# Moving the low parts of a split-precision matmul 64 bytes aside in on-chip memory

## The chip, the core and the metric

The kernel runs on one core of one Trainium2 chip. The metric is the time of one execution on the device, in microseconds (us); less is better. Float32 products are made on TensorE out of three cheaper passes each, so that TensorE is used far more than the arithmetic alone would ask.

## The reference

A "macaron" block on x of 4096 tokens by 256 channels: half of a feed-forward part, a retention part with 8 heads, and the same feed-forward part again, each behind a layer norm and added to its input.

```python
def ffn(x):                       # x: layer-normed, 4096 x 256
    x_prev = shift_by_one_token(x)
    xr = mu_r * x + (1 - mu_r) * x_prev
    xk = mu_k * x + (1 - mu_k) * x_prev
    r = sigmoid(xr @ W_r.T)
    k = relu(xk @ W_k.T) ** 2
    return r * (k @ W_v.T)

x = x + 0.5 * ffn(layernorm(x))
x = x + retention(layernorm(x) @ Wq, ... @ Wk, ... @ Wv) @ Wo   # causal, decay per head
x = x + 0.5 * ffn(layernorm(x))
```

## The kernel before

**Blocks and stages.** The tokens are cut into 16 blocks of 256 (two tiles of 128). Each block goes through the stages FFN1, RET and FFN2. The stages of different blocks run at the same time: in the loop `for i in range(6, 16)` TensorE works on FFN1 of blocks i-2 and i-1, on RET of i-4 and i-3 and on FFN2 of i-6 and i-5. The order of the work on every engine is written out by hand; one pass of that loop is called an iteration here.

**Splitting.** A float32 operand `a` is stored as `a_hi` (rounded to float32r, the format of the three passes) and `a_lo = a - a_hi`. ScalarE (ACT) writes the high parts, VectorE (DVE) and GpSimd (POOL) the low parts. One product is the sum of three passes: high by high, low of one by high of the other, high by low. The weights are split once, at the start.

**The two forms of a product.** Every matmul has an operand that is loaded into the array first (the stationary one, a LDWEIGHTS of 128 columns, engine PEld in the profile) and one that is streamed through it (256 columns). Both are float32 in memory, so a load reads 512 bytes of each partition and a stream 1024.
- `half_T` (line 1097) loads the weight `w` and streams the operand `x`. It makes `hidden`, `query` and `key`.
- `half_rows` (line 1105) loads `x` and streams `w`. It makes `gate`, `ffn_out`, `value` and `retention_out`.

Each call of either is a run of six matmuls: two halves `g` of the contraction, three passes each. Calls of one form often follow each other, so that the trace shows runs of 6 or 12.
Behind "psum<-" the profile prints the streamed operand first and the loaded one second: `psum<-xa_hi,w_hi` streams `xa_hi` through `w_hi`.

**The first and the last block.** Block 0 of FFN1 and block 15 of FFN2 (and its output projection of retention) use plain float32 matmuls on `w_f32`, `xkT`, `xrT`, `sqT` and `o_last` (lines 1268 to 1315). Line 1330 is a warm-up on a tensor of zeros, which it loads and streams; line 1334 is a run of ten matmuls that load and stream `w_hi` and keep the clock up near the end.

**Where the tensors lie.** `sb` allocates them one behind another in a partition's memory, in the order of the declarations, each at the next multiple of 32 bytes. The sizes are multiples of 128 bytes for all large tensors but `xnT` (2056 bytes); small ones between them move what follows. Added up from the declarations, the start addresses are, modulo 128 bytes:

| tensors | before | after the change |
|---|---|---|
| `w_f32`, `w_hi` | 0 | 0 |
| `w_lo` | 0 | 64 |
| `ident`, `zeros`, `decay`, `decq`, `deck` | 32 | 96 |
| `x0`, `x1`, `x2`, `y` | 0 | 64 |
| `xn`, `dT`, `xkT`, `xrT`, `sqT`, `qT`, `kT`, `vrow`, `krow`, `attn`, `o_last` | 64 | 0 |
| `xk_hi`, `xr_hi`, `ka_hi`, `xa_hi`, `o_hi` | 64 | 64 |
| `xk_lo`, `xr_lo`, `ka_lo`, `xa_lo`, `o_lo` | 64 | 0 |

Of the kernel before, what the change touches and what calls it, by code (L numbers as in the profile page):

```python
# [8 lines left out]
F32R = mybir.dt.float32r  # L9
# [5 lines left out]
G = D // P  # L15
TILES = 2
BT = TILES * P
# [7 lines left out]
def build(nc, x_in, weights, mu_in, ident_in, decay_in, decq_in, deck_in, gstate_in, x_out):  # L25
# [5 lines left out]
    with ExitStack() as ctx:  # L31
        def sb(name, shape, dt=F32):
            return ctx.enter_context(nc.sbuf_tensor(name, [P] + shape, dt))

        def ring(name, count, shape, dt=F32):

            return [sb(f"{name}_{k}", shape, dt) for k in range(count)]
# [11 lines left out]
        W_R, W_K, W_V, W_Q, W_KEY, W_VAL, W_O = range(7)  # L49
        w_f32 = [sb(f"w_f32_{w}", [G, D]) for w in range(7)]  # L50
        w_hi = [sb(f"w_hi_{w}", [G, D], F32R) for w in range(7)]
        w_lo = [sb(f"w_lo_{w}", [G, D], F32R) for w in range(7)]
        mu = sb("mu", [2, G])
        ident = sb("ident", [P])
# [25 lines left out]
        def ffn(name, count, shape, dt=F32):  # L80
            return {f: ring(f"{name}_{f}", count, shape, dt) for f in (FFN1, FFN2)}
# [1 line left out]
        xnT = ffn("xnT", 2, [G, BT + 1])  # L83
        dT = ffn("dT", 2, [G, BT])
        xkT, xrT = ffn("xkT", 2, [G, BT]), ffn("xrT", 2, [G, BT])
        xk_hi, xk_lo = ffn("xk_hi", 2, [G, BT], F32R), ffn("xk_lo", 2, [G, BT], F32R)
        xr_hi, xr_lo = ffn("xr_hi", 2, [G, BT], F32R), ffn("xr_lo", 2, [G, BT], F32R)
        reluT, sqT = ffn("reluT", 1, [G, BT]), ffn("sqT", 1, [G, BT])
        ka_hi, ka_lo = ffn("ka_hi", 1, [G, BT], F32R), ffn("ka_lo", 1, [G, BT], F32R)
        rgate, gatedx = ffn("rgate", 1, [TILES, D]), ffn("gatedx", 1, [TILES, D])  # L90


        xa_hi, xa_lo = sb("xa_hi", [G, BT], F32R), sb("xa_lo", [G, BT], F32R)
        qT, kT = sb("qT", [G, BT]), sb("kT", [G, BT])
        vrow, krow = sb("vrow", [TILES, D]), sb("krow", [TILES, D])
        attn = [sb(f"attn_{r}", [G, TILES, P]) for r in range(HG)]
        state = [sb(f"state_{c}", [G, HD]) for c in range(TILES)]
        state_dec = [sb(f"state_dec_{c}", [G, HD]) for c in range(TILES)]
        o_hi, o_lo = sb("o_hi", [G, BT], F32R), sb("o_lo", [G, BT], F32R)

        o_last = sb("o_last", [G, BT])

        psum = ctx.enter_context(nc.psum_tensor("psum", [P, 8, 512], F32))
        bank = [psum[:, b, :] for b in range(8)]

        def halves(b):
            return bank[b].rearrange("p (g t) -> p g t", g=2)
# [73 lines left out]
        def signal(whole, name, f, part):  # L181
            return half_done[name] if part == 0 else whole[f]
# [37 lines left out]
        def splits(f, n):  # L220

            return max(n - 1, 0) if f == FFN1 else n
# [859 lines left out]
        def _(pe):  # L1082
# [9 lines left out]
            def half_T(b, w, hi, lo, m):  # L1092

                cols = slice(m * P, (m + 1) * P)
                passes = [(w_hi[w], hi), (w_lo[w], hi), (w_hi[w], lo)]
                for j, (g, (wt, xt)) in enumerate([(g, p) for g in range(G) for p in passes]):
                    mm = pe.matmul(halves(b)[:, m, :], wt[:, g, cols], xt[:, g, :], start=(j == 0), stop=(j == 5))  # L1097
                return mm
# [9 lines left out]
            def weight_split(n, w):  # L1108

                if n == 0 or (n == 1 and w in (W_R, W_K, W_V)):  # L1110
                    pe.wait_ge(w_hi_ready[w], 1)
                    pe.wait_ge(w_lo_ready[w], 1)

            def hidden(f, n, half):
                if half == 0:
                    pe.wait_ge(xk_lo_ready[f], splits(f, n + 1))
                    weight_split(n, W_K)
                mm = half_T(B_HID[f], W_K, xk_hi[f][n % 2], xk_lo[f][n % 2], half)
                if half == 1:
                    mm.then_inc(hid_psum[f], 1)  # L1120
# [17 lines left out]
            def query(n, half):  # L1138
                if half == 0:
                    pe.wait_ge(xa_lo_ready, n + 1)  # L1140
                    weight_split(n, W_Q)
                mm = half_T(B_Q, W_Q, xa_hi, xa_lo, half)
                if half == 1:
                    mm.then_inc(q_psum, 1)

            def key(n, half):
                if half == 0:
                    pe.wait_ge(xa_lo_ready, n + 1)
                    weight_split(n, W_KEY)
                mm = half_T(B_KEY, W_KEY, xa_hi, xa_lo, half)  # L1150
                if half == 1:
                    mm.then_inc(key_psum, 1)
# [79 lines left out]
            def hidden_in_parts(f, n, step):  # L1232

                g = min(step, 1)
                pe.wait_ge(signal(xk_lo_ready, "xk_lo", f, g), splits(f, n + 1) if g != 0 else 1)
                if step == 0:
                    weight_split(n, W_K)
                hi, lo = xk_hi[f][n % 2], xk_lo[f][n % 2]
                for m in range(2) if step == 0 else [step - 1]:
                    b, cols = (B_HID_1[f] if m else B_HID[f]), slice(m * P, (m + 1) * P)  # L1240
                    for j, (wt, xt) in enumerate(((w_hi[W_K], hi), (w_lo[W_K], hi), (w_hi[W_K], lo))):
                        mm = pe.matmul(halves(b)[:, m, :], wt[:, g, cols], xt[:, g, :], start=(g == 0 and j == 0), stop=(g == 1 and j == 2))
                if step > 0:
                    mm.then_inc(signal(hid_psum, "hid", f, step - 1), 1)
# [504 lines left out]
```

## Time and profile before

| | |
|---|---|
| median of 3 runs | 336.15 us (335.98 to 336.43) |
| the profiled execution's own time | 336.06 us |
| its span, from the first to the last instruction | 334.3 us |
| TensorE (PE) busy | 323.9 us (97%) |
| weight loads (PEld) busy | 303.2 us (91%) |
| VectorE (DVE) busy | 298.0 us (89%) |
| ScalarE (ACT) busy | 206.4 us (62%) |
| GpSimd (POOL) busy | 136.5 us (41%) |

The span is what the engines' records cover; the execution's own time holds some 1.8 us more around it. A matmul's record starts when its streaming starts and ends after its results have passed the array, so records of consecutive matmuls overlap, and PE is "busy" whenever one of them is in flight. What one matmul costs is therefore the distance from its start to the next one's, not its duration. The granted clock of TensorE was 1.000 over the span.

### The profile page before, as it was taken

Reading aid. Unit: us, or ns where it says so; the run is one execution under the profiler, and the core shown is the slowest. Engines: PE = TensorE matmul, PEld = TensorE weight load, DVE = VectorE, ACT = ScalarE, POOL = GpSimd, SP = SyncE. Lnnn points to the kernel's source line nnn. Section 1 sums busy time; section 2 is a strip of 40 time slices with the busy share of each in tenths; the row PEclk is TensorE's granted clock in tenths of the full one; section 3 lists DMA queues with packets and bytes.
Section 4 is the critical chain, followed back from the end, with each engine's and each line's share of the span. In section 5 each row is a group of like instructions: output and inputs, shape, how many; then the busy total and the mean of one; then the engine's idle time right before and its main releaser. Section 6 shows DMA issues by size and latency. Waiting matters only on the chain.

```text
span 334.3 us, 11273 instructions
## 1 busy us (share of the span) xinstructions
PE 323.9 (97%) x4252; PEld 303.2 (91%) x4252; DVE 298.0 (89%) x699; ACT 206.4 (62%) x414; POOL 136.5 (41%) x242
## 2 busy tenths in 40 slices
PE   7889999999999999999999999999999999999995
PEld 7679989999899999999999999989999999999893
DVE  4998899999998999899999989999997989888883
ACT  3685665774757586575758657575866738164542
POOL 3476563708153350716345070634516114333320
PEclk9999999999999999999999999999999999999999
DMA  7611010102002010200202020011001000000001
GB/s 243 240 35 33 3 31 3 35 2 64 4 1 65 2 65 4 63 4 3 64 2 64 4 64 2 10 58 34 2 2 34 2 33 4 31 2 33 5 31 63
DMA packets 11556, 12.08 MB, mean 36 GB/s; under 512 B 1008, under 2 KB 11120, under 8 KB 11504
## 3 DMA queue, kind: packets, MB, share of 16 engines
q1 hardware_dynamic: 11072, 11.18, 10.7%
q8 instruction: 34, 0.56, 0.7%
q10 hardware_dynamic: 432, 0.20, 0.2%
q14 instruction: 18, 0.15, 0.1%
HBM read 7.18 MB, written 4.19 MB: 34 GB/s over the span
## 4 chain that ended last, share of the span: by engine, by line
PE 90%; DVE 5%; issue 2%; ACT 0%; POOL 0%; DVEq 0%; ACTq 0%; POOLq 0%
PE psum L1105 39%; PE psum L1097 26%; PE psum L1089 6%; PE psum L1176 5%; PE psum L1208 5%; PE psum L1195 3%; PE psum L1166 2%; PE psum L1221 2%; PE psum L1298 2%; DVE xrT L800 1%; DVE w_lo L175 1%; PE psum L1315 1%; PE psum L1279 1%; DVE dT L780 0%; DVE state_dec L845 0%
## 5 line engine op out<-in xcount | busy, mean ns | idle before, releaser
L234 POOL TENSOR_TENSOR xr_lo<-xrT,xr_hi 128x512 fp32r<-128x512 f32 x27 | 45.4, 1695 | 118.9 <-ACT xr_hi L427 118.9
L396 ACT ACTIVATE xn<-x,shift,rstd 128x256 f32<-128x256 f32 x92 | 49.7, 590 | 2.7 <-POOL shift L323 2.6
L836 DVE TENSOR_TENSOR attn<-psum,decay 128x512 f32<-128x512 f32 x64 | 42.2, 683 | 6.6 <-PE psum L1176 5.9
L466 ACT ACTIVATE kT<-psum 128x512 f32<-128x512 f32 x16 | 9.6, 598 | 51.9 <-PE psum L1097 51.9
L1105 PE MATMUL psum<-w_hi,xr_hi 128*128 128x256 f32 x120 | 37.6, 314 | 0.5 <-issue 0.5
L700 DVE BATCH_NORM_STATS2 stats<-x 128x6 f32<-128x256 f32 x94 | 34.9, 413 | 3.5 <-DMA x<-in_x 3.4
L1097 PE MATMUL psum<-xa_hi,w_hi 128*128 128x256 f32 x128 | 36.4, 284 | 0.4 <-DVE xa_lo L814 0.3
L1097 PE MATMUL psum<-xa_lo,w_hi 128*128 128x256 f32 x128 | 35.6, 278 | 0.0
L1097 PE MATMUL psum<-xa_hi,w_lo 128*128 128x256 f32 x128 | 35.6, 278 | 0.0
L1105 PE MATMUL psum<-w_hi,ka_hi 128*128 128x256 f32 x120 | 35.4, 295 | 0.1
L319 POOL TENSOR_TENSOR rstd<-var_eps,exponent 128x2 f32<-128x2 f32 x47 | 33.4, 710 | 3.7 <-DVE var_eps L711 3.7
L1097 PE MATMUL psum<-xk_hi,w_hi 128*128 128x256 f32 x120 | 34.7, 289 | 0.2 <-issue 0.2
L1105 PE MATMUL psum<-w_hi,ka_lo 128*128 128x256 f32 x120 | 33.6, 280 | 0.0
L1105 PE MATMUL psum<-w_hi,xr_lo 128*128 128x256 f32 x120 | 33.6, 280 | 0.0
L1105 PE MATMUL psum<-w_lo,ka_hi 128*128 128x256 f32 x120 | 33.6, 280 | 0.0
L1105 PE MATMUL psum<-w_lo,xr_hi 128*128 128x256 f32 x120 | 33.5, 279 | 0.0
L1097 PE MATMUL psum<-xk_lo,w_hi 128*128 128x256 f32 x120 | 33.3, 278 | 0.0
L1097 PE MATMUL psum<-xk_hi,w_lo 128*128 128x256 f32 x120 | 33.2, 277 | 0.0
L1089 PE MATMUL psum<-ident,xn 128*128 128x128 f32 x188 | 28.2, 273 | 2.0 <-DVE xn L717 1.0
L435 ACT ACTIVATE reluT<-psum 128x512 f32<-128x512 f32 (+1 forms) x32 | 18.7, 584 | 17.5 <-PE psum L1097 16.1
L800 DVE SCALAR_TENSOR_TENSOR xrT<-dT,mu,xnT 128x256 f32<-128x256 f32 x62 | 29.0, 508 | 0.0
L315 POOL TENSOR_TENSOR var_eps<-moments,eps 128x2 f32<-128x2 f32 x46 | 16.7, 363 | 25.0 <-DVE moments L706 24.3
(122 smaller groups left out, 1040.7 us busy)
## 6 DMA issues: line engine op xcount, KB each, us to landing
x<-in_x SPq DMA_DIRECT2D x15, 256.0 KB, 2.9
x_out<-y SPq DMA_DIRECT2D x15, 256.0 KB, 3.0
w_f<-in_w SPq DMA_DIRECT2D x7, 256.0 KB, 6.1
decay<-in_decay SPq DMA_DIRECT2D x1, 512.0 KB, 6.8
decq<-in_decq SPq DMA_DIRECT2D x1, 256.0 KB, 6.5
deck<-in_deck SPq DMA_DIRECT2D x1, 256.0 KB, 6.5
x_out<-y SPq DMA_DIRECT2D x2, 128.0 KB, 1.7
x<-in_x ACTq DMA_DIRECT2D x1, 128.0 KB, 2.8
```

Source lines behind the costliest of these rows:

```text
L234: engine.tensor_tensor(xr_lo[f][n % 2][:], xrT[f][n % 2][:], xr_hi[f][n % 2][:].bitcast(F32), ALU.subtract).then_inc(xr_lo_ready[f], 1)
L319: pool.tensor_tensor(rstd[s][n % 2][:], var_eps[s][n % 2][:], exponent[:], ALU.pow).then_inc(rstd_ready[s], 1)
L396: act.activation(xn[s][n % 2][:, t, :], x[n % len(x)][:, t, :], ACT.Identity, bias=shift[s][n % 2][:, t:t + 1], scale=rstd[s][n % 2][:, t: ...
L435: act.activation(reluT[f][0][:, s, :], halves(b)[:, s, :], ACT.Relu).then_inc(signal(relu_ready, "relu", f, part), 1)
L700: dve.bn_stats(stats[s][n % 2][:, t, :], x[n % len(x)][:, t, :]).then_inc(stats_ready[s], 1)
L800: dve.scalar_tensor_tensor(out=xrT[f][n % 2][:, g, :], in0=dT[f][n % 2][:, g, :], scalar=mu[:, 0, g:g + 1], in1=xnT[f][n % 2][:, g, 0:BT], ...
L836: dve.tensor_tensor(attn[r][:], bank[B_SCORES[r]].rearrange("p (g c i) -> p g c i", g=G, c=TILES), decay[:, r, :, :].unsqueeze(2).broadcas ...
L1089: mm = pe.transpose(halves(B_T[s])[:, g, t * P:(t + 1) * P], xn[s][n % 2][:, t, g * P:(g + 1) * P], ident[:])
L1097: mm = pe.matmul(halves(b)[:, m, :], wt[:, g, cols], xt[:, g, :], start=(j == 0), stop=(j == 5))
L1105: mm = pe.matmul(halves(b)[:, t, :], xt[:, g, cols], wt[:, g, :], start=(j == 0), stop=(j == 5))
L1176: mm = pe.matmul(bank[B_SCORES[r]][:, group * P:(group + 1) * P], kT[rows, g, c * P:(c + 1) * P], qT[rows, g, c * P:(c + 1) * P], start=Tr ...
L1208: mm = pe.matmul(bank[B_OT + g][quadrant(g, r), c * P:(c + 1) * P], vrow[:, c, cols], attn[r][:, g, c, :], start=(first and c == 0), stop= ...
```

## The change

Three pads of 64 bytes (`gap_lo`, `gap_hi`, `gap_split`) are put between declarations, and the high and low parts of the operands are declared together, behind everything else. All `w_lo` then start 64 bytes off `w_hi`, and all operands' low parts 64 bytes off their high parts. In `half_T` and in `hidden_in_parts` the pass with `w_lo` comes first. The number of instructions and their sizes stay as they are.

```diff
         w_hi = [sb(f"w_hi_{w}", [G, D], F32R) for w in range(7)]
+
+        gap_lo = sb("gap_lo", [16])
         w_lo = [sb(f"w_lo_{w}", [G, D], F32R) for w in range(7)]
...
-        xk_hi, xk_lo = ffn("xk_hi", 2, [G, BT], F32R), ffn("xk_lo", 2, [G, BT], F32R)
-        xr_hi, xr_lo = ffn("xr_hi", 2, [G, BT], F32R), ffn("xr_lo", 2, [G, BT], F32R)
         reluT, sqT = ffn("reluT", 1, [G, BT]), ffn("sqT", 1, [G, BT])
-        ka_hi, ka_lo = ffn("ka_hi", 1, [G, BT], F32R), ffn("ka_lo", 1, [G, BT], F32R)
...
-        xa_hi, xa_lo = sb("xa_hi", [G, BT], F32R), sb("xa_lo", [G, BT], F32R)
...
-        o_hi, o_lo = sb("o_hi", [G, BT], F32R), sb("o_lo", [G, BT], F32R)
 
         o_last = sb("o_last", [G, BT])
+
+
+        gap_hi = sb("gap_hi", [16])
+        xk_hi, xr_hi, ka_hi = ffn("xk_hi", 2, [G, BT], F32R), ffn("xr_hi", 2, [G, BT], F32R), ffn("ka_hi", 1, [G, BT], F32R)
+        xa_hi, o_hi = sb("xa_hi", [G, BT], F32R), sb("o_hi", [G, BT], F32R)
+        gap_split = sb("gap_split", [16])
+        xk_lo, xr_lo, ka_lo = ffn("xk_lo", 2, [G, BT], F32R), ffn("xr_lo", 2, [G, BT], F32R), ffn("ka_lo", 1, [G, BT], F32R)
+        xa_lo, o_lo = sb("xa_lo", [G, BT], F32R), sb("o_lo", [G, BT], F32R)
...
             def half_T(b, w, hi, lo, m):
 
                 cols = slice(m * P, (m + 1) * P)
-                passes = [(w_hi[w], hi), (w_lo[w], hi), (w_hi[w], lo)]
+                passes = [(w_lo[w], hi), (w_hi[w], hi), (w_hi[w], lo)]
...
-                    for j, (wt, xt) in enumerate(((w_hi[W_K], hi), (w_lo[W_K], hi), (w_hi[W_K], lo))):
+                    for j, (wt, xt) in enumerate(((w_lo[W_K], hi), (w_hi[W_K], hi), (w_hi[W_K], lo))):
```

## Rows read from the trace of the kernel before

**Rows 1.** The page, part 1: busy time of each engine, its share and instructions.

```profile
PE 323.9 (97%) x4252; PEld 303.2 (91%) x4252; DVE 298.0 (89%) x699; ACT 206.4 (62%) x414; POOL 136.5 (41%) x242
```

**Rows 2.** The page, part 4: the chain that ended last, by engine.

```profile
PE 90%; DVE 5%; issue 2%; ACT 0%; POOL 0%; DVEq 0%; ACTq 0%; POOLq 0%
```

**Rows 3.** Busy time in three windows: stretch, its length, engine busy (instructions).

```profile
0.00:64.40 64.40, 58.54 (x666) 53.52 (x666) 54.86 (x137) 39.25 (x78) 34.57 (x69) 1.00 0.26 81
64.40:278.70 214.30, 214.30 (x2910) 202.97 (x2906) 199.60 (x468) 141.67 (x285) 85.81 (x151) 1.00 0.09 26
278.70:334.30 55.60, 51.03 (x681) 46.68 (x680) 43.53 (x97) 25.50 (x53) 16.11 (x24) 1.00 0.07 25
```

**Rows 4.** The chain in time order, one iteration: start us, us, engine, line, count.

```profile
142.49 0.91 PE psum L1105 x6
...
143.84 1.38 PE psum L1105 x12
...
146.25 0.90 PE psum L1105 x6
...
148.16 0.88 PE psum L1105 x6
149.05 1.36 PE psum L1097 x12
150.41 1.42 PE psum L1105 x12
151.82 0.71 PE psum L1097 x6
152.53 0.69 PE psum L1105 x6
153.23 0.68 PE psum L1097 x6
153.91 1.42 PE psum L1105 x12
155.32 1.42 PE psum L1097 x12
156.74 0.44 PE psum L1089 x4
157.18 0.71 PE psum L1105 x6
157.89 0.68 PE psum L1097 x6
...
159.01 0.69 PE psum L1097 x6
159.69 0.71 PE psum L1105 x6
```

**Rows 5.** The same view near the end: the run of line 1334.

```profile
320.95 1.20 PE psum L1334 x10
```

**Rows 6.** Whole span, line 1105 alone, then line 1097: stretch, PE, PEld.

```profile
0.00:334.30 334.30, 156.00 (x1092) 136.23 (x1092) 1.00 0.12 36
...
0.00:334.30 334.30, 101.27 (x744) 91.98 (x744) 1.00 0.12 36
```

**Rows 7.** Waits of DVE within the iteration: us in total, times, longest.

```profile
DVE krow L829 <- PE psum L1166: 0.3, 1, 0.3
DVE attn L836 <- PE psum L1176: 0.2, 1, 0.2
```

**Rows 8.** Timeline: start us, us, engine; a matmul and the load beside it.

```profile
150.72 0.28 PE L1105 MATMUL psum<-w_lo,ka_hi 128*128 128x256 f32 x1
150.72 0.19 PEld L1105 LDWEIGHTS psum<-w_hi,ka_lo 128*128 128x128 f32 x1
```

**Rows 9.** Timeline near the start: the warm-up of line 1330.

```profile
7.00 1.73 PE L1330 MATMUL psum<-zeros 128*128 128x128 f32 x14
```

## The prediction

> **What bounds the kernel now.** I read the page first. PE is busy for 323.9 of 334.3 us [rows 1], and the chain that ended last is PE for 90% [rows 2]. Busy PE is no proof of PE at its peak, so I cut the span into a beginning, a middle and an end: in the middle, 64.4 to 278.7 us, PE is in flight for every one of the 214.30 us, while before and after it has gaps, 58.54 of 64.40 and 51.03 of 55.60 us [rows 3]. The middle repeats: the same piece of the chain comes back each 19.40 us, 214.30 / 19.40 = 11.05 iterations. So the time of the middle is the number of matmuls times the distance between their starts, and nothing that another engine does counts until PE has to wait for it.
>
> What a matmul costs is then the thing to read, and the chain in time order gives it for each run: its pieces go from one matmul's end to the next one's [rows 4]. The reader is to see that there are two paces for the very same shapes. The run of 12 at 149.05 takes 1.36 us, 0.1133 each; the run of 12 at 150.41 takes 1.42 us, 0.1183 each. I call them the short and the long pace. Neither belongs to one form: line 1097 (w loaded) has the short one at 149.05, 153.23 and 157.89 and the long one at 151.82 and 155.32; line 1105 (w streamed) the short one at 152.53 and the long one at 153.91. A pace lasts over a boundary from 1105 to 1097: 148.16 to 149.05 short, 150.41 to 151.82 long, 152.53 to 153.23 short, 153.91 to 155.32 long; 157.18 to 157.89 is the exception. At every boundary from 1097 straight to 1105 it turns over: 149.05 to 150.41 short to long, 151.82 to 152.53 long to short, 153.23 to 153.91 and 159.01 to 159.69 short to long [rows 4].
>
> Now the addresses. While matmul k streams, the load for k+1 reads; both start together, as at 150.72 [rows 8]. Before the change all w parts start at 0 modulo 128 and all x parts at 64. Inside a run one of them is streamed and the other loaded, so the two start in different halves of 128 bytes. Only at a boundary between the forms do both start in the same half: (64, 64) from 1097 to 1105, (0, 0) from 1105 to 1097. The pace turns over just where the pair is (64, 64). And the one run in which streamed and loaded operand are the same bytes throughout, line 1334, goes at 1.20 / 10 = 0.120 us each, the longest of all for this shape [rows 5]. That is the evidence that the half matters. It is no proof: at (0, 0) boundaries the pace mostly stays.
>
> **What the change does to this.** With the new addresses and pass order the pairs (streamed, next loaded) are, for 1097, (hi 64, w_hi 0), (hi 64, w_hi 0), (lo 0, w_lo 64), and for 1105 (w_hi 0, hi 64), (w_lo 64, lo 0), (w_hi 0, hi 64). At the boundaries 1097 ends with lo at 0 and 1105 begins with hi at 64; 1105 ends with w_hi at 0 and 1097 begins with w_lo at 64. So the start halves differ in every pair, at the boundaries too. Inside runs they differed before, so nothing is won there directly. What I expect to go is the turn-over at boundaries.
>
> The price, per iteration, against 0.68 per six [rows 4]: 150.41 gives back 0.06, 151.82 0.03, 152.53 0.01, 153.91 0.06, 155.32 0.06, 159.69 0.03, together 0.25 us. All six lie behind a turn-over; without it they inherit the short pace that 148.16 and 159.01 have. The long starts behind other kinds of matmul have no such cause and I leave them as they are: 142.49 and 146.25 (0.91 and 0.90 against 0.88 at 148.16, so 0.03 and 0.02), 143.84 (0.02), 157.18 (0.03), together 0.10 us. The rows are rounded to 0.01, so either sum may be 0.03 off.
>
> Times how many iterations: lines 1105 and 1097 have 1092 + 744 = 1836 such matmuls [rows 6], at 120 in an iteration 15.3 iterations' worth. 11.05 of them are in the middle, where PE never waits and every saved nanosecond counts. The other 4.25 lie at the ends, where PE is in flight for 91% of the time and part of a saving goes into waits; between a half and 0.91 I take 0.7, which is 3.0. That makes 14.0 iterations, and 0.25 x 14.0 = 3.5 us.
>
> The rest I cost at nothing, with these bounds. **The cover:** a faster PE brings nearer what DVE owes it. In the iteration DVE waits for PE for 0.3 + 0.2 = 0.5 us [rows 7]; that is how far an iteration can shrink before DVE's order sets it, and 0.25 is half of it. If PE gained more, the next thing late would be DVE's scores and key rows, and PE would begin to wait for attn and xa_lo. **The plain float32 matmuls** of the first and last blocks (64 instructions) now stream and load from one half, where they had two. At worst each loses what line 1334 loses against the short pace, 0.120 - 0.1133 = 0.007, in all 0.4 us; but the warm-up, which loads and streams the same zeros, goes at about (1.73 - 0.28) / 13 = 0.112 us [rows 9], for 128 columns of plain float32, no more than 256 columns of a pass take here, so I see no price for a same-half pair there. I take 0. **Pairs among the other tensors** (transposes, scores, retention) move by 64 bytes together and keep their relative places: 0. **The pass order** only swaps two loads, and both weight parts are waited for before the run in any case: 0. **Vector, scalar and DMA work** sees starts that are moved by 64 bytes; DVE's 0.5 us and the loads issued blocks ahead cover it: 0.
>
> Sum: the profiled execution would take 336.06 - 3.5 = 332.6 us; it lies 0.09 us under the median of the runs, so the median would be 336.15 - 3.5 = 332.6 us.
>
> **Rules that speak against it.** PE is slowed by something between its two readers, as the two paces for one shape show [rows 4]. The Trainium skill says otherwise: "TensorE: Matmul & The Clock Gate", section "Step-by-step: what each phase is for", gives TensorE two independent read ports, one for the streamed operand and one for the loads, and "SBUF — State Buffer", section "SBUF: two separate sides", has contention only on the port pair that VectorE and GpSimd share. By that rule a move of 64 bytes changes nothing and the time stays 336.15 us; it leaves the two paces unexplained, so I give it little.
>
> **The rivals.**
> - *Every run gets the short pace*, those behind other kinds of matmul too (0.35 per iteration). For it: those starts may depend on the same halves. Against it: their first pairs are as before. 0.35 x 14.0 = 4.9 us, 331.3 us. Chance 0.10.
> - *A pace under 0.1133.* Transposes go at 0.44 / 4 = 0.110 [rows 4]. If 0.1133 still holds a conflict, 120 x 0.0033 = 0.4 us more per iteration would come free, 0.75 in all, above DVE's 0.5 us, which caps it: 0.5 x 14.0 = 7 us, 329.1 us. Against it: the halves inside runs differ already. Chance 0.06.
> - *The alternation costs something.* Now the half of the streamed operand changes inside runs. 152.53, right behind a change, has 0.01 over 153.23; at 0.01 for each six, 20 times an iteration, 0.2 of the 0.25 is eaten: 0.05 x 14.0 = 0.7 us, 335.5 us. Chance 0.10.
> - *Nothing changes*: the pace is set by the relative timing in which a run starts, and addresses 64 bytes apart are no matter. For it: the exception at 157.18 and the (0, 0) boundaries. 336.15 us. Chance 0.09.
> - *Slower.* What turns the pace over is not the equal halves but the move of the streamed operand from one half to the other; at 1097 to 1105 it goes from 64 to 0. Then the change puts such a move into every group of three passes, and the long pace prevails. Of the 120 matmuls of an iteration 66 are at the long pace now; it decides against the change from more than 66 on. With all of them there, the other 54 lose 0.005 each, 0.27 us, times 14.0: 3.8 us, 339.9 us; at line 1334's pace 120 x 0.0067 - 0.35 = 0.45 us, 342.5 us. Against it: from 0 to 64, at 1105 to 1097, the pace stays. Chance 0.21, a third of it under 338.
>
> **How the numbers follow.** My own case (turn-overs gone, 332.6 us) has the remaining 0.44. A run of this kernel can be told from no change above some 0.2%, 0.7 us. Faster by more: 0.44 + 0.10 + 0.06 + half of the eaten gain, 0.05, makes 0.65. Within 0.2%: 0.05 + 0.09 = 0.14. Slower: 0.21. The range goes from 331.0 us, just under the case of all runs short with the rounding of its sum, to 338.0 us; outside are the lower pace (0.06) and two thirds of the slower case (0.14). My own case alone spans 331.9 to 333.3 us: the rounding of its sum, 0.03 x 14, and the share taken at the ends, 0.5 to 0.91.
>
> **What the profile after would show.** The chain in time order again: if I am right, the runs that answer to those at 150.41, 151.82, 153.91, 155.32 and 159.69 take 0.68 per six and not 0.71, those at 142.49, 146.25 and 157.18 stay, and an iteration takes 19.15 us and not 19.40, with PE still without waits. DVE's waits for PE shrink by some 0.25 us. If all runs show 0.71 or more, the slower case holds; if the long ones are as many but elsewhere, the pace is a matter of timing. If a pace under 0.68 appears, look for PE's waits on DVE. I would be wrong above all if the state at which a run starts is set by something that the new addresses move as well, since one short or long start is then inherited by nine runs behind it.

## The result and the profile after

The changed kernel takes 339.25 us (median of 4 runs, 338.92 to 339.37) against 336.29 us for the kernel before beside it: a ratio of 1.0083, 95% interval 1.0070 to 1.0096. It is slower by 0.8%. The forecast was 332.6 us, with a range up to 338.0; the time lies above it. Ratios compare undisturbed executions: one of the 11 of the run `pads_256` below took 453.43 us at a granted clock of 0.657 and has no part in its ratio.

The profiled execution took 339.33 us, its span is 337.5 us, 3.2 more than before. In the windows of the three parts and of one iteration (stretch, length, busy time of PE, PEld, DVE, ACT and POOL), the middle has grown most, and PE is still in flight for all of it, as in [rows 3]. An iteration takes 19.63 us and not 19.40:

```profile
0.00:65.00 65.00, 59.83 (x694) 54.74 (x698) 55.30 (x137) 39.56 (x79) 34.85 (x69) 1.00 0.25 80
65.00:281.50 216.50, 216.50 (x2902) 205.22 (x2888) 199.50 (x467) 141.47 (x284) 85.54 (x151) 1.00 0.09 25
281.50:337.50 56.00, 51.53 (x681) 47.13 (x680) 43.50 (x97) 25.48 (x53) 16.23 (x24) 0.99 0.07 25
143.26:162.89 19.63, 19.63 (x268) 18.64 (x264) 18.24 (x43) 12.95 (x28) 8.00 (x15) 1.00 0.10 28
```

The chain in time order of that iteration answers, run by run, to [rows 4] (line 1110 is 1105 of before, 1102 is 1097, 1094 is 1089):

```profile
143.72 0.92 PE psum L1110 x6
...
145.08 1.41 PE psum L1110 x12
...
147.53 0.91 PE psum L1110 x6
...
149.44 0.92 PE psum L1110 x6
150.36 1.42 PE psum L1102 x12
151.78 1.41 PE psum L1110 x12
153.19 0.71 PE psum L1102 x6
153.90 0.70 PE psum L1110 x6
154.61 0.71 PE psum L1102 x6
155.32 1.41 PE psum L1110 x12
156.73 1.42 PE psum L1102 x12
...
158.59 0.71 PE psum L1110 x6
159.29 0.71 PE psum L1102 x6
...
160.44 0.72 PE psum L1102 x6
161.16 0.70 PE psum L1110 x6
```

There is no run of 0.68 left. The reader can add up where the time went, after minus before: 143.72 +0.01, 145.08 +0.03, 147.53 +0.01, 149.44 +0.04, 150.36 +0.06, 151.78 -0.01, 153.90 +0.01, 154.61 +0.03, 155.32 -0.01, 159.29 +0.03, 160.44 +0.03, 161.16 -0.01, the others 0. That is 0.22 us of the 0.23 by which the iteration grew. Ten iterations in a row take 19.627 us each, 0.227 more than 19.40, and 0.227 times the 14.0 iterations of the prediction is 3.2 us, all of the span's growth. What ran at the long pace still does; everything that ran at the short one has lost it.

### The profile page after: what moved, and what is told of

It reads as the page before. It is cut to its first block, busy times and chain, and to the rows that moved or that the text cites. A ratio compares the mean times of both kernels' runs of the same rounds, so it can differ in the third digit from the quotient of the medians.

```text
span 337.5 us, 11273 instructions
## 1 busy us (share of the span) xinstructions
PE 327.9 (97%) x4252; PEld 307.1 (91%) x4252; DVE 298.3 (88%) x699; ACT 206.5 (61%) x414; POOL 136.6 (40%) x242
## 4 chain that ended last, share of the span: by engine, by line
PE 91%; DVE 5%; issue 2%; ACT 0%; POOL 0%; DVEq 0%; POOLq 0%; ACTq 0%
PE psum L1110 39%; PE psum L1102 26%; PE psum L1094 6%; PE psum L1181 5%; PE psum L1213 4%; PE psum L1200 3%; PE psum L1171 2%; PE psum L1226 2%; PE psum L1303 2%; DVE w_lo L180 1%; PE psum L1320 1%; PE psum L1284 1%; DVE xrT L805 1%; DVE stats L705 0%; DVE state_dec L850 0%
## 5 line engine op out<-in xcount | busy, mean ns | idle before, releaser
L1102 PE MATMUL psum<-xa_hi,w_lo 128*128 128x256 f32 x128 | 36.7, 287 | 0.4 <-DVE xa_lo L819 0.4
L1102 PE MATMUL psum<-xk_hi,w_lo 128*128 128x256 f32 x120 | 35.2, 293 | 0.2 <-issue 0.2
L1102 PE MATMUL psum<-xk_hi,w_hi 128*128 128x256 f32 x120 | 33.7, 281 | 0.0
```

## The experiments

**Theories.** A, that of the prediction: a matmul is held up when streamed and next loaded operand start in one half of 128 bytes. B: it is held up when the streamed operand moves from one half to the other between matmuls. C: the pace is set by timing, by waits and the other engines. D, which came up after experiment 5: the short pace needs an operand pair that keeps its places, modulo 256 bytes, from matmul to matmul.

**1. The parts of the change.** The pads and declarations of the change with the old pass order, and the new pass order on the old layout:

```diff
 # pads_only: the changed kernel, but
-                passes = [(w_lo[w], hi), (w_hi[w], hi), (w_hi[w], lo)]
+                passes = [(w_hi[w], hi), (w_lo[w], hi), (w_hi[w], lo)]
 # (and the same in hidden_in_parts); order_only: the reverse edit on the kernel before
```

> The pads and declarations of the change, with the passes of before (w_hi first). In the weight-loading form the pairs of streamed and next loaded start are then (hi 64, w_lo 64), (hi 64, w_hi 0), (lo 0, w_hi 0): two of three in one half. Theory A, equal halves cost time: slower than the change, 341 to 343 us. Theory B, what costs is that the streamed operand moves from one half to the other between matmuls, whatever the pair: moves inside runs as in the change, so the same as the change, 339 us.

> The pass order of the change on the old addresses; start halves are as before, inside runs and at boundaries. Theories A and B both: no difference to before, 336.2 us, with the short and the long pace in the same places. If this alone is slower, the order of the passes is the cause.

`pads_only` took 338.33 us, ratio 1.0070 (1.0053 to 1.0087); `order_only` 335.80 us, ratio 0.9995 (0.9985 to 1.0006). The pass order alone, on the old layout, is nothing, and the addresses carry most of the loss. The chains show iterations of 19.55 and 19.40 us; first `pads_only`, then `order_only`, each with the pieces that open two iterations in a row:

```profile
142.03 0.39 PE psum L1226 x32
...
161.58 0.39 PE psum L1226 x32
```

```profile
141.90 0.39 PE psum L1221 x32
...
161.30 0.39 PE psum L1221 x32
```

So the pass order that the change adds, and that makes every pair unlike, costs 0.08 us an iteration on top of the pads, where A had it save. A expected 341 us or more for `pads_only`, B the change's 339; it lies under both, nearer to B.

**2. No operand ever moves, every pair in one half.**

```diff
 # one_half: the kernel before, and
+        gap_split = sb("gap_split", [16])
         xk_hi, xk_lo = ffn("xk_hi", 2, [G, BT], F32R), ffn("xk_lo", 2, [G, BT], F32R)
```

> The kernel before with one pad of 64 bytes ahead of xk_hi: all weights and all operands then start at 0 modulo 128, every pair lies in one half, and no operand ever moves to the other half. Theory A, equal halves cost: the long pace or 0.120 us everywhere, 340 to 343 us. Theory B, moves between halves cost: no move is left, the short pace everywhere, 331 to 332 us.

339.92 us, ratio 1.0114 (1.0099 to 1.0129). B, by itself, is refuted: without any move the time is longer still. Equal places do cost; A has that right. The size is that of a lost short pace and little more: in its chain an iteration takes 19.69 us and its runs of twelve 1.42 or 1.43 us, 0.119 each, not the 0.120 of line 1334.

**3. The pace by itself.** A kernel that runs rows of one pair over and over, then rows of changing pairs:

```python
PATTERNS = [              # (streamed, loaded), start modulo 128
    constant(0, 0), constant(0, 16), ..., constant(0, 112),
    constant(64, 0), constant(64, 64), constant(32, 96), constant(96, 32), ...
    runs((64, 0, 12), (0, 64, 12), (64, 0, 12), (0, 64, 12), ...),   # both swap at a run's end
    runs((64, 0, 12), (0, 0, 1), (0, 64, 11), (64, 64, 1), ...),     # swap, no pair in one half
    [(64, 64), (64, 0), (0, 0)] * 8,    # the changed kernel's passes, w loaded
    [(0, 64), (64, 64), (0, 0)] * 8, ]  # and w streamed
```

> Not the reference's work: x is copied to the output, and TensorE runs rows of 24 to 72 matmuls of 128 loaded and 256 streamed columns with chosen start addresses, each row twice, behind transposes and behind small matmuls. Theory A: constant pairs in different halves go at 0.1133 us, those in one half at 0.118 to 0.120; rows in which both operands alternate but never share a half go at 0.1133. Theory B: all constant pairs go at one pace, 0.1133, and every row with a streamed operand that moves goes at 0.118. In the row with swaps at each end of a run of 12 but no pair in one half, A expects no turn-over of the pace, B expects one.

In the timeline of PE (start, us, streamed and loaded tensor, count) `sa`, `sc`, `se`, `sg` are streamed from 0, 32, 64, 96 modulo 128, and `la`, `lc`, `le`, `lg` loaded from there. Of each row the first matmul takes some 0.2 us and the record of the last one reaches 0.28 us past its start:

```profile
18.74 3.12 PE L77 MATMUL psum<-sa,la 128*128 128x256 f32 x24
...
25.33 3.08 PE L77 MATMUL psum<-sa,lc 128*128 128x256 f32 x24
...
31.88 3.07 PE L77 MATMUL psum<-sa,le 128*128 128x256 f32 x24
...
51.60 2.99 PE L77 MATMUL psum<-sc,lg 128*128 128x256 f32 x24
...
77.65 1.66 PE L77 MATMUL psum<-se,la 128*128 128x256 f32 x12
79.15 1.54 PE L77 MATMUL psum<-sa,le 128*128 128x256 f32 x12
80.53 1.53 PE L77 MATMUL psum<-se,la 128*128 128x256 f32 x12
81.89 1.58 PE L77 MATMUL psum<-sa,le 128*128 128x256 f32 x12
83.31 1.58 PE L77 MATMUL psum<-se,la 128*128 128x256 f32 x12
...
133.59 3.00 PE L77 MATMUL psum<-sa,le 128*128 128x256 f32 x24
```

Less the first 0.20 and the last 0.28, the 22 steps between take 2.64 us for the pair (0, 0), 0.120 each; 2.60 for (0, 32), 0.118; 2.59 for (0, 64), 0.118; but 2.51 for (32, 96), 0.114. And the very same pair (0, 64) is long at 31.88 and short at 133.59: of the 3.00 us there, 0.22 are the first and 0.12 a long second matmul, which leaves 2.38 for 21, 0.1133. So (0, 64) has two paces and keeps whichever it fell into. The half of 128 bytes is not what sorts the rows: (0, 32) lies in one half and has 0.118, and (0, 112), with unlike halves, has a record of 3.13 us, as long as that of (0, 0); (0, 0) and (64, 64) are among the longest both times. What does is whether the loaded operand starts above or below the streamed one. Of the 18 constant rows (some load from places up to 576), each run twice, the short pace came for (32, 96) and (0, 576) both times and for (0, 64) and (0, 320) once: in all four the loaded operand starts 64 bytes above the streamed one modulo 256. Where it starts 64 below, in (64, 0), (96, 32) and (0, 192), all six were long, with records of 3.08 to 3.10 us. The row of swaps from 77.65 shows the turn-over of [rows 4] while no other engine works: the distances from start to start are 1.38 and 1.36 us for the second and third 12 (0.115 and 0.113), 1.42 (0.118) for the fourth.

The rows that answer to the change's own passes decide. In the chain they are the pieces of 24 that start at 92.79 (w loaded) and 96.04 (w streamed):

```profile
92.79 2.81 PE psum L77 x24
...
96.04 2.83 PE psum L77 x24
```

That is 0.117 and 0.118 each, with no pair in one half, where A had 0.1133. A falls. In the row with swaps but no pair in one half, the first time no turn-over came (its three runs of 11, from 88.07, 89.48 and 90.90, have records of 1.46 us each). The second time one came at each swap (from 214.13, 215.49 and 216.91 the records are 1.41, 1.46 and 1.41 us). So equal halves are not what turns the pace over either.

**4. TensorE's order of one iteration, without waits, on ten layouts.**

```python
VARIANTS = [   # starts modulo 2048 of w_hi, w_lo, x_hi, x_lo; of other tensors, ident; new pass order
    ((128, 128, 960, 960), 64, 32, False),   # before
    ((128, 192, 64, 128), 0, 96, True),   # after
    ((128, 128, 1024, 1024), 0, 32, False),   # one half
    ((128, 128, 64, 64), 64, 32, False), ... ]   # x at 64, 192, 320, 448, 576, 704, 832
```

> Not the reference's work: x is copied to the output, and TensorE alone goes through the kernel's order of one iteration (120 matmuls of the three-pass products, transposes, scores, retention) three times for each of ten layouts, with no waits. Theory A (the pace follows from the addresses and the order of the matmuls alone): the layout of before takes 19.40 us an iteration, that of the change 19.63, that with all in one half as much as in the run one_half, and the seven others, with weights at 128 and operands at 64, 192, 320, 448, 576, 704 or 832 modulo 1024, all 19.40, if only the half counts. Theory C (the pace is set by timing, by what waits and other engines do): 19.40 and 19.63 don't come back here. If the layouts with the same halves differ among each other, bits of the address above 128 count as well.

The pieces of the chain that open two iterations in a row, for before and after:

```profile
39.70 0.39 PE psum L107 x32
...
59.16 0.39 PE psum L107 x32
...
98.20 0.39 PE psum L107 x32
...
117.83 0.39 PE psum L107 x32
```

The layout of the change gives 19.63 us, that of one half 19.67 (19.69 in the real kernel, by its chain), that of before 19.41 in its first iteration and 19.46 in the next two. So PE's own stream of addresses gives the changed kernel's iteration to 0.01 us and that of before to 0.06, and 0.17 to 0.22 us of the 0.23 that an iteration lost; theory C, waits and the other engines, is not needed for these. x at 64, 320, 576 or 832 gave 19.37, at 192, 448 or 704 gave 19.46: the half of 128 is the same in all, a place modulo 256 is not.

With x at 64 the steps at which the pace turns over are the others. In this chain line 77 is 1105 of the kernel (w streamed) and line 72 is 1097 (w loaded):

```profile
224.17 1.36 PE psum L77 x12
225.54 0.71 PE psum L72 x6
226.25 0.71 PE psum L77 x6
226.95 0.69 PE psum L72 x6
```

Short to long and long to short now come from line 1105 to 1097, where the pair is (0, 0), and at (64, 64), from 1097 to 1105, the pace stays. So it is not the pair (64, 64) that turns it over. In both layouts it is the step into the form whose loaded operand starts 64 bytes above the streamed one modulo 256; the run at 157.18 of [rows 4] and the second row of such swaps in experiment 3 have turn-overs at the other step too, so this is a rule with exceptions.

**5. Forty layouts and pass orders.** `iter2` is the same program over sixteen ways to put each of the four parts at one of two places 128 bytes apart, and four with the weights moved by 32 to 96; `iter3` has the new pass order and all other orders of the three passes.

> As iter1 (TensorE alone, x copied to the output), two iterations for each of twenty layouts in the old pass order: w_hi, w_lo, x_hi and x_lo each at one of two places 128 bytes apart modulo 256, operands 64 off the weights, and four layouts with the weights moved by 32, 64 or 96 as well. If only the half of 128 bytes counts, all give 19.37 to 19.46 us an iteration; if a layout exists that keeps the short pace over the boundaries, it shows 19.07, which is 19.40 less the 0.33 that the long pace costs in the chain of before.

> As iter2: eight layouts with the low-part pass first where w is loaded, then the layout w 128, x 64 (19.37 us in iter1) with every order of the three passes in either form, then the pads of the change with the old order, the old layout with the new order, and one with the other tensors moved. Theory A (addresses and order alone): the pads with the old order take as long as an iteration of the run pads_only, the new order on the old layout 19.40 to 19.46. No theory here says which order is best; one under 19.2 us would be worth building.

No layout came under 19.36 us in an iteration that another one followed, and the 19.07 of a layout that keeps the short pace was not found. With high and low parts at the same place the iterations took 19.36 to 19.50 us; with x_lo 128 bytes off x_hi, 19.48 to 19.75; with w_lo alone 128 off, 19.46 to 19.62. Unlike halves are kept in all of these. D gives no sizes: w_lo 128 off gave 19.46 and 19.47 in two of its four layouts, no more than the layout of before has in experiment 4, and 19.58 to 19.62 in the others. The ten other pass orders gave 19.44 to 19.46 us where the old one has 19.37 to 19.40; the pads of the change with the old order 19.54 and 19.59, which is `pads_only`.

**6. How far aside, and how often the pace turns over.** Layouts with x at 64, low parts moved by 256, by 512, by 64 for the weights alone, by 64 for the operands alone and by 32; then the order of the next experiment.

> As iter1 (TensorE alone, x copied to the output), three iterations for each of ten cases. Theory D (the short pace lives only as long as streamed and loaded operand keep their places modulo 256 from matmul to matmul; a low part that lies elsewhere breaks it every third matmul): low parts moved by 256 or 512 bytes leave 19.37 us, moved by 32 or 64 bytes, of the weights alone or of the operands alone, give 19.5 to 19.65. Theory A' (only the half of each pair counts): only layouts with pairs in one half are longer. With the grouped order (the two halves of three products side by side, so that the long pace is left after 12 matmuls and not after 42) on the old layout: 19.26 us instead of 19.40, if the pace turns over at each step from the weight-loading to the weight-streaming form; on the layout of the change no difference to 19.63, because there is no short pace to hold.

The chain of `iter4`, the openings of the second and third iteration of four layouts: low parts 256 aside, weights' low parts 64 aside, operands' low parts 64 aside, and all 32 aside:

```profile
98.64 0.39 PE psum L112 x32
...
118.02 0.39 PE psum L112 x32
...
215.09 0.39 PE psum L112 x32
...
234.68 0.39 PE psum L112 x32
...
273.91 0.39 PE psum L112 x32
...
293.54 0.39 PE psum L112 x32
...
332.74 0.39 PE psum L112 x32
...
352.30 0.39 PE psum L112 x32
```

19.38 and 19.37 us for 256 and 512, which is what the same layout takes with low and high parts at one place; 19.59, 19.63 and 19.56 for the others. That is D: what the change lost is the sameness of places, and either side alone loses nearly all of it. Between D and A' only 32 aside decides, which has no pair in one half, beside the change itself and the layouts with x_lo 128 off; with one side 64 aside one pair in three starts in one half, so that both theories have these two longer.

The grouped order missed its forecast here. On the layout of before its iterations took 19.29, 19.38 and 19.38 us, against 19.46 for the old order and 19.26 forecast; with x at 64 it took 19.40, against 19.37 for the old order; on the layout of the change 19.62 and 19.63, as forecast.

**7. The same pads, 256 bytes wide, in the real kernel.**

```diff
 # pads_256: the changed kernel, but
-        gap_lo = sb("gap_lo", [16])
+        gap_lo = sb("gap_lo", [64])     # likewise gap_hi and gap_split
```

> The whole change, its pass order too, with pads of 256 bytes where it has 64: low parts lie 256 bytes aside, so that modulo 256 all operands keep the places of before. Theory D (places modulo 256 that stay from matmul to matmul hold the short pace): an iteration of 19.40 to 19.46 us and the time of before, 336.0 to 336.8. If it were the moving aside as such, or the order of the declarations, it would take the change's 339.

336.08 us, ratio 0.9993 (0.9982 to 1.0005). Everything else of the change is in this kernel, its pass order, its declarations, three pads; only the 64 is gone, and so is the loss. An iteration takes 19.40 us. The chain has the 0.88 and 1.36 of [rows 4] again:

```profile
148.56 0.88 PE psum L1110 x6
149.44 1.36 PE psum L1102 x12
```

**8. Fewer turn-overs: a version that beats both.** If the pace turns over at each step from 1097 to 1105, the length of the runs between two such steps decides how many matmuls are long. On the old layout, the loop's order is changed so that 12 matmuls and not 42 lie behind an odd step:

```diff
                 ffn_out(FFN2, i - 6, 0)
+                ffn_out(FFN2, i - 6, 1)
                 pe.wait_ge(xa_lo_ready, i - 2)
                 key(i - 3, 0)
...
-                ffn_out(FFN2, i - 6, 1)
                 pe.wait_ge(attn_ready[0], i - 3)
                 ffn_out(FFN1, i - 2, 0)
                 query(i - 3, 1)
                 pe.wait_ge(o_lo_ready, i - 3)
                 retention_out(i - 4, 0)
-                pe.wait_ge(gate_ready[FFN1], i - 1)
-                hidden(FFN2, i - 5, 0)
                 retention_out(i - 4, 1)
                 ffn_out(FFN1, i - 2, 1)
+                pe.wait_ge(gate_ready[FFN1], i - 1)
+                hidden(FFN2, i - 5, 0)
                 key(i - 3, 1)
```

> The kernel before, its layout untouched; in the loop the second half of ffn_out(FFN2), of retention_out and of ffn_out(FFN1) move up and the first half of hidden(FFN2) down, so that the steps from the weight-loading to the weight-streaming form lie 12 matmuls apart and not 18 and 24. If the pace turns over at these steps, 30 matmuls an iteration go from 0.1183 to 0.1133 us: 19.26 us an iteration and some 1.5 us less in all, 334.6. If the pace has another cause (waits, the units beside PE), no change or a new wait, 336.2 or more.

334.76 us, ratio 0.9964 (0.9949 to 0.9979), 0.4% under the kernel before. Its chain in time order, the part that was regrouped:

```profile
147.62 1.56 PE psum L1105 x12
149.19 1.36 PE psum L1097 x12
150.55 0.71 PE psum L1105 x6
151.26 0.71 PE psum L1097 x6
151.97 2.05 PE psum L1105 x18
154.02 2.04 PE psum L1097 x18
```

Twelve at the long pace (0.71 per six), then 36 at the short one (2.05 / 18 = 0.114, 2.04 / 18 = 0.1133), as forecast; the iteration takes 19.27 us where 19.26 was expected and the replay of experiment 6 had 19.38. On top of the change the same regrouping should gain nothing:

> The grouped order of the loop on top of the change. Theory D: no short pace to hold, so the 1.0 to 1.5 us that grouping gave on the old layout don't come: an iteration of 19.63 us as in iter4, 339 us. If grouping helped by other means (waits, work of other engines), it gives the same 0.13 us an iteration here: 19.50 us and 337.5.

338.91 us, ratio to the kernel before 1.0092 (1.0074 to 1.0110): no gain, so what `grouped` wins is the pace. The profiled execution took 340.67 us at a granted clock of 0.948, with iterations of 19.66 to 19.70 us, so the 19.63 is not to be read there. The replay of this case in `iter4`, at a clock of 1.000, has it, and its runs of 18 take 2.12 and 2.13 us, where `grouped` has 2.05 and 2.04.

## Why the prediction was wrong

**What bounds the kernel: right.** PE is in flight for the whole middle in every run here, and the loss is PE's. The count of 14.0 iterations, with 0.7 of the ends, agrees: 0.227 x 14.0 = 3.2 us, the span's growth. So do the costs taken as nothing, but for one. The matmuls of line 1334 take 1.20 us for ten in the changed kernel too, as in [rows 5], and the warm-up 1.73 us for 14, as in [rows 9], and the last twelve plain float32 products 2.61 us in both kernels. In the iteration DVE waits for PE as before (0.3 us for `krow`, 0.3 for `attn`), and PE waits for nothing. The one is the pass order: by itself it measured 0.9995, but on top of the pads it costs 0.08 us an iteration (experiment 1), 0.08 x 14.0 = 1.1 us, a third of the loss, where the prediction had 0.

**The step that failed** is the one of the 0.25 us: "All six lie behind a turn-over; without it they inherit the short pace that 148.16 and 159.01 have." There was nothing to inherit. The runs that answer to these two became long themselves (149.44, 0.92 for 0.88; 160.44, 0.72 for 0.69). Behind it stood the reading that a pair of unlike halves is the same to TensorE whichever operand lies in which half, so that nothing changes inside the runs. Experiments 3, 4, 6 and 7 put in its place: inside the runs is where it is lost. Three passes whose operands change places every few matmuls go at 0.117 to 0.118 us even if no pair ever shares a half, and with low parts 256 aside an iteration keeps its 19.37 us.

**The evidence for equal halves was half of the matter.** That equal places cost was read rightly from line 1334's 0.120 us: all at one place modulo 128 costs 1.1% (experiment 2). But the turn-over at (64, 64) was taken for its effect. It is tied to the swap: it came with a swap and no equal pair (in one of two rows), and with x moved by 128 bytes the pace turns over at (0, 0) and stays at (64, 64) (experiment 4). One row of [rows 4] showed this already: from 157.18 to 157.89 the pace turned at a pair (0, 0). It was set aside as "the exception".

**Which rival came true.** "Slower", put at 0.21, has the right place and size: all 54 short matmuls of an iteration long, 339.9 us forecast, 339.25 measured. Its mechanism, a move of the streamed operand between halves, is half right: such moves between the passes of a run end the short pace, but so do moves by 32 bytes and mostly by 128, and a layout without any move can be longer still. The range left out two thirds of this case. "Nothing changes" was refuted, and with it the rule of independent ports in the Trainium skill ("TensorE: Matmul & The Clock Gate", "Step-by-step: what each phase is for"): experiment 2 moves nothing but addresses and adds 1.1% to the kernel before, and experiment 7 moves nothing but addresses and takes away the 0.8% of the change, so here the measurement decides against it. How the two readers get in each other's way, no run shows.

**What stays open.** Why a constant pair has two paces, and what picks the one it starts with, is not settled: the pair (0, 64) fell into either, and the layout of before takes 19.41 us in one iteration and 19.46 in the next of experiment 4. Nor is it known why some moves by 128 bytes cost little, or by what the pass order costs time. That the period is 256 bytes rests on the layouts tried, most of them with weights at 128 and operands at eight places.

## What to carry to other kernels

- A rule drawn from the boundaries between runs has to be checked inside the runs: before moving operands, write down the pair of addresses of every matmul, before and after, and ask which of them the trace has shown in that sequence. None of the change's sequences was in the trace of before.
- Where high and low parts of a split are streamed and loaded in turns, keep them at the same place modulo 256 bytes (the width tried here) and the two operands 64 apart; and try runs of one form side by side, as a pace of 0.1133 or 0.118 us is inherited from run to run: it won 0.4% in the kernel before, nothing on the layout of the change, and in the replay with x at 64 it lost 0.03 us an iteration.
- PE's stream alone, replayed with no waits, gave an iteration to 0.01 us for the change, 0.06 for the kernel before and 0.11 for `grouped`, so a winner of a replay has still to be run. Layouts can be compared so by the dozen in one execution.

## What the runs showed of the hardware

The pace of matmuls with 128 loaded and 256 streamed float32r columns depends on start addresses in on-chip memory: 0.1133, about 0.118 or 0.120 us at a granted clock of 1.000. It has a memory: the same pair ran at 0.118 in one row and at 0.1133 in another of the same execution, and each held to the row's end. In constant rows the short pace came only where the loaded operand starts 64 bytes above the streamed one modulo 256, six rows of eight, and never where it starts 64 below, none of six. An iteration of the real kernel, 19.40 us, came out the same with low parts beside or 256 bytes aside, and 0.23 us longer with them 64 aside.
